# The end of an attention and quantised-feed-forward layer on one core: tiles moved ahead of the last values, and rounding and addition shared differently between GpSimd and VectorE

## What is computed

```python
def _quant_per_tensor(x):
    scale = jnp.maximum(jnp.max(jnp.abs(x)) / QMAX, EPS)
    q = jnp.clip(jnp.round(x / scale), -QMAX, QMAX).astype(jnp.int8)
    return (q, scale)
...
h = _dyn_quant_linear(hidden_state, w1, b1)
h = jax.nn.gelu(h, approximate=False)
return _dyn_quant_linear(h, w2, b2)
```

## Time and profile before

| what | value |
|---|---|
| median of 3 runs | 736.91 us |
| the profiled execution's own time | 732.62 us |
| its span, first to last instruction | 730.8 us |
| mean granted TensorE clock | 0.944 of full speed |
| busy: PE, DVE, ACT, POOL | 86%, 73%, 63%, 65% |
| last values done | about 675.8 us |
| first Gelu starts, last maximum ends | 677.56, 702.70 us |
| first rounding starts | 704.08 us |
| last addition on GpSimd ends | 728.17 us |

### The profile page before, as it was taken

How to read it: one execution, slowest core, us unless ns; L and a number is a source line. 1 busy time by engine, 2 the same in 40 slices (tenths; PEclk the granted TensorE clock), 3 DMA queues, 4 the chain that set the end, 5 groups by cost and what they waited for, 6 DMA issues and landing times.

```text
span 730.8 us, 15856 instructions
## 1 busy us (share of the span) xinstructions
PE 630.3 (86%) x6282; PEld 489.4 (67%) x6282; DVE 532.5 (73%) x822; ACT 461.5 (63%) x715; POOL 476.4 (65%) x256
## 2 busy tenths in 40 slices
PE   7989878878899899989987998789899988974956
PEld 5666656667686687667765776678677866863635
DVE  6746789766668786878677777676778777873896
ACT  3466746667657675767676667665677667663754
POOL 2488599775665887579768577855777778610225
PEclk9798998989999999999999999999899999997889
DMA  9866776688987988799888878888788888886003
GB/s 255 262 208 193 179 126 125 122 157 154 205 150 134 180 159 136 148 191 166 145 139 153 138 135 150 160 134 159 140 151 139 132 132 141 134 142 127 15 1 115
DMA packets 326680, 108.34 MB, mean 148 GB/s; under 512 B 308880, under 2 KB 317648, under 8 KB 326480
## 3 DMA queue, kind: packets, MB, share of 16 engines
q1 hardware_dynamic: 325824, 106.75, 75.5%
q10 hardware_dynamic: 784, 0.59, 0.3%
HBM read 21.30 MB, written 10.49 MB: 43 GB/s over the span
## 4 chain that ended last, share of the span: by engine, by line
PE 30%; DVE 28%; ACT 13%; DMA 12%; issue 11%; POOL 5%; SPq 1%; POOLq 0%; DVEq 0%; ACTq 0%
PE psum L1059 28%; DVE small L862 12%; DMA pt<-p_src 9%; ACT psum L678 7%; DVE p_src L870 5%; ACT p_src L672 3%; DMA acc<-in_L_attn_x 2%; ACT o_hi L660 2%; DVE o_lo L894 2%; DVE hid L1039 1%; DVE small L1008 1%; POOL res L533 1%; DVE acc L761 1%; DVE acc L900 1%; DVE o_norm L887 1%
## 5 line engine op out<-in xcount | busy, mean ns | idle before, releaser
L672 ACT ACTIVATE p_src<-psum,small 128x1024 f16<-128x1024 f32 (+7 forms) x256 | 183.4, 742 | 190.4 <-DVE small L862 189.8
L862 DVE TENSOR_REDUCE small<-psum 128x1 f32<-128x1024 f32 (+7 forms) x256 | 186.7, 750 | 58.6 <-PE psum L1059 58.4
L870 DVE TENSOR_TENSOR p_src<-psum,p_src 128x1024 f16<-128x1024 f32 (+2 forms) x192 | 182.5, 951 | 32.3 <-ACT psum L678 31.9
L1059 PE MATMUL psum<-kv_tok,pt 128*128 128x65 f16 (+1 forms) x3456 | 146.6, 198 | 52.5 <-DMA pt<-p_src 38.5
L1059 PEld LDWEIGHTS psum<-kv_tok,pt 128*128 128x128 f16 x3456 | 124.1, 100 | 97.2 <-issue 68.7
L678 ACT ACTIVATE psum<-psum,small 128x1024 f32<-128x1024 f32 (+7 forms) x256 | 178.2, 719 | 0.0
L1059 PE MATMUL psum<-k_hi,q_hi 128*128 128x512 f32 (+2 forms) x384 | 161.0, 419 | 15.8 <-POOL q_lo L484 6.3
L466 POOL TENSOR_TENSOR q_swap<-q_raw,sin_sb 32x1024 f32<-32x1024 f32 x32 | 75.9, 2373 | 119.4 <-ACT q_raw L606 118.9
L1059 PE MATMUL psum<-k_hi,q_lo 128*128 128x512 f32 (+2 forms) x384 | 134.7, 351 | 0.0
L1059 PE MATMUL psum<-k_lo,q_hi 128*128 128x512 f32 (+2 forms) x384 | 134.4, 350 | 0.0
L1059 PEld LDWEIGHTS psum<-k_hi,q_hi 128*128 128x128 f32 x384 | 76.5, 199 | 23.8 <-issue 11.1
(11 more groups left out here) (160 smaller groups left out, 918.5 us busy)
## 6 DMA issues: line engine op xcount, KB each, us to landing
pt<-p_src SPq DMA_TRANSPOSE x384, 3.3
wq_split<-w_split SPq DMA_DIRECT2D x4, 1024.0 KB, 5.0
k_rotated<-k_split SPq DMA_DIRECT2D x8, 512.0 KB, 3.4
wq<-wq_split SPq DMA_DIRECT2D x16, 256.0 KB, 3.4
acc<-in_L_attn_x SPq DMA_DIRECT2D x4, 512.0 KB, 7.9
ffn_t<-in_L_attn_W_o SPq DMA_DIRECT2D x1, 2048.0 KB, 19.5
k_hi<-k_rotated SPq DMA_DIRECT2D x8, 256.0 KB, 3.9
k_lo<-k_rotated SPq DMA_DIRECT2D x8, 256.0 KB, 4.6
```

Of the source, the lines that this page charges most:

```text
L672: ins = act.activation(p_src[u][:, 0, at:at + w], psum[:, COLS[i]:COLS[i] + w], ACT.Exp, bias=nb)
L862: dve.tensor_reduce(sm["mcol"][:, NT * (n % 2) + i:NT * (n % 2) + i + 1], psum[:, COLS[i]:COLS[i] + (i + 1) * P], AX.X, ALU.max, negate=True)\
L870: dve.tensor_tensor(p_src[u][:, 1, :], psum[:, o:o + WIDE[u]], p_src[u][:, 0, :], ALU.subtract)\
L1059: ins = pe.matmul(dst, lhs, rhs, start=start, stop=stop, skip_group_check=True)
```

## The change

- **Order of the tiles.** Half 0 first, c = 0 to 7, then half 1. The loop on TensorE now ends after iteration n = 31. The values of units 0 and 1 of the last step come first, then tile 0; units 2, 3, 4 and 5 come behind tiles 0, 2, 4 and 6 (`VALUES_BEHIND`), tile 0 of the queries behind tile 6. `normalise` of the last step is done after maximum 6 (`HEADS_AT`), together with the two small `dg` products. The last `turn_pair`s stand behind tiles 8 and 9 (were 0 and 1), the output products behind tiles 11, 12, 13, 14 (were 4, 6, 8, 10). Banks are given per tile, bank 5 only from tile 10 on. ScalarE waits for `att_pool` and `att_sp` before Gelu 0 (was Gelu 6).
- **Taking MAGIC off.** Parts (0,1) and (1,1) go from VectorE to GpSimd, behind its eight b2 additions.
- **Addition of `acc`.** GpSimd keeps the even results u, VectorE adds the odd ones itself, right behind their multiplication.

```diff
-OUT_AT = {4: 0, 6: 1, 8: 2, 10: 3}
-DVE_QUANT = {(0, 1), (1, 1)}
-FFN_ORDER = [(1, c) for c in (2, 3, 4, 5, 6, 7, 0, 1)] + [(0, c) for c in range(8)]
-FFN_BANKS = (0, 2, 5)
+OUT_AT = {11: 0, 12: 1, 13: 2, 14: 3}
+TURN_AT = {8: 0, 9: 1}
+VALUES_BEHIND = {0: 2, 2: 3, 4: 4, 6: 5}
+HEADS_AT = 6
+POOL_QUANT = {(0, 1), (1, 1)}
+FFN_ORDER = [(h, c) for h in range(2) for c in range(8)]
+FFN_BANKS = (0, 2, 6, 0, 2, 6, 0, 2, 0, 2, 5, 0, 2, 5, 0, 2)
...
+        def first_head(m):
+            return first_of_head if m + 1 < LAST else bank[4][:, 0:VC]
...
-                sp.wait_ge(S["f_res"], u + 1)
+                sp.wait_ge(S["f_res_dve" if u % 2 else "f_res"], u // 2 + 1)
...
             pool.wait_ge(S["f_bias"], TT // 2)
-            for u in range(TT // 2):
+            for i, (t, hf) in enumerate(sorted(POOL_QUANT)):
+                pool.wait_ge(S["f_round"], 2 * t + hf + 1)
+                cs = slice(4 * hf, 4 * hf + 4)
+                pool.tensor_scalar(hqs[t % 2][:, cs, :], hid_quarter(t)[:, cs, :], -MAGIC, None, ALU.add)\
+                    .then_inc(S["f_quant_pool"], 1)
+                pool.wait_ge(S["f_quant_pool"], i + 1)
+            for u in range(0, TT // 2, 2):
...
-                if i == 6:
+                if i == 0:
                     for s in ("att_pool", "att_sp"):
                         act.wait_ge(S[s], 1)
-                if i < 2:
-                    turn_high(1, i, MISC_END + i)
+                if i in TURN_AT:
+                    turn_high(1, TURN_AT[i], MISC_END + TURN_AT[i])
...
-                    if n and j == NS - 1:
+                    if 0 < n < LAST and j == NS - 1:
                         normalise(n - 1, False)
-            normalise(LAST - 1, True)
-            for k in range(2):
-                dve.tensor_scalar(dg[:, k, :], identf[:, :], sm["w2s"][:, k:k + 1], None, ALU.mult).then_inc(S["f_dg"], 1)
             for i in range(16):
                 dve.wait_ge(S["f_gelu"], i + 1)
                 ins = dve.tensor_reduce(sm["hmax"][:, i:i + 1], hid[:, FFN_ORDER[i][0], FFN_ORDER[i][1], :], AX.X, ALU.max,
                                        apply_absolute_value=True)
-                if i < 2:
-                    turn_low(1, i, TURNS[LAST] + i + 1, MISC_END + i)
+                if i == HEADS_AT:
+                    normalise(LAST - 1, False)
+                    normalise(LAST - 1, True)
+                    for k in range(2):
+                        dve.tensor_scalar(dg[:, k, :], identf[:, :], sm["w2s"][:, k:k + 1], None, ALU.mult)
+                if i in TURN_AT:
+                    turn_low(1, TURN_AT[i], TURNS[LAST] + TURN_AT[i] + 1, MISC_END + TURN_AT[i])
...
                 dve.tensor_tensor(res[u % RES][:, :, :], bank[u % 4].rearrange("p (t n) -> p t n", n=D), s2_row[:, :, :],
                                   ALU.mult).then_inc(S["f_mul"], 1)
+                if u % 2:
+                    dve.wait_ge(S["f_mul"], u + 1)
+                    dve.wait_ge(S["f_bias"], TT // 2)
+                    t = 4 * QUARTERS[u // 2] + 2 * (u % 2)
+                    y = res[u % RES]
+                    dve.tensor_tensor(y[:, :, :], y[:, :, :], acc[:, t:t + 2, :], ALU.add).then_inc(S["f_res_dve"], 1)
...
                     dve.tensor_scalar(h, h, sm["rsh"], MAGIC, ALU.mult, ALU.add).then_inc(S["f_round"], 1)
-                    if (t, hf) in DVE_QUANT:
-                        dve.wait_ge(S["f_round"], 2 * t + hf + 1)
-                        dve.tensor_scalar(hqs[t % 2][:, 4 * hf:4 * hf + 4, :], h, -MAGIC, None, ALU.add)\
-                           .then_inc(S["f_quant_dve"], 1)
...
-            for n in range(LAST + 1):
+            for n in range(LAST):
...
-            pe.wait_ge(S["lo_done"], NS * LAST)
+            for u in range(2):
+                values(LAST - 1, u)
             for i in range(16):
                 half, c = FFN_ORDER[i]
-                if i >= 3:
-                    pe.wait_ge(S["f_gelu"], i - 2)
-                if i == 2:
-                    pe.wait_ge(S["misc6_used"], BANK_OF.count(6))
+                taken = [k for k in range(i) if abs(FFN_BANKS[k] - FFN_BANKS[i]) < 2]
+                if i < 2:
+                    pe.wait_ge(S["lo_done"], NS * LAST - (2 if i == 0 else 0))
+                if i == 1:
+                    pe.wait_ge(S["head_read"], 2 * (LAST - 1))
+                if taken:
+                    pe.wait_ge(S["f_gelu"], taken[-1] + 1)
+                if i == FFN_BANKS.index(6):
+                    for b in (6, 7):
+                        pe.wait_ge(S[f"misc{b}_used"], BANK_OF[:MISC_END].count(b))
+                if i == FFN_BANKS.index(5):
+                    pe.wait_ge(S["head_read"], 2 * LAST)
...
-                if i < 2:
-                    turn_pair(i, MISC_END + i, 2 * end)
+                if i in VALUES_BEHIND:
+                    values(LAST - 1, VALUES_BEHIND[i])
+                    if i == HEADS_AT:
+                        first_values(LAST - 1)
+                if i in TURN_AT:
+                    pe.wait_ge(S["f_gelu"], 6)
+                    turn_pair(TURN_AT[i], MISC_END + TURN_AT[i], 2 * end)
```

More of the change, by code:

```diff
@@ L255, in build @@
             pool_step qhi_done qlo_done o_hi_done norm_step
-            att_pool att_sp f_quant_dve
-            f_psum f_gelu f_max f_hrow f_hall f_step f_att f_bias f_round f_quant f_out f_mul f_res f_s2 f_dg f_dgps""".split()
+            att_pool att_sp f_quant_pool
+            f_psum f_gelu f_max f_hrow f_hall f_step f_att f_bias f_round f_quant f_out f_mul f_res f_res_dve f_s2 f_dg f_dgps""".split()
         S = {n: sem(n) for n in names}
@@ L712, in _ @@
                 act.wait_ge(S["f_psum"], i + 1)
-                if i == 6:
+                if i == 0:
                     for s in ("att_pool", "att_sp"):
                         act.wait_ge(S[s], 1)
-                first = FFN_BANKS[i % 3] * CH
+                first = FFN_BANKS[i] * CH
                 act.activation(hid[:, half, c, :], psum[:, first:first + 2 * CH], ACT.Gelu,
                                scale=sm["s1"][:, c:c + 1], bias=sm["b1"][:, c:c + 1]).then_inc(S["f_gelu"], 1)
-                if i < 2:
-                    turn_high(1, i, MISC_END + i)
+                if i in TURN_AT:
+                    turn_high(1, TURN_AT[i], MISC_END + TURN_AT[i])
             for t in range(4):
                 for hf in range(2):
-                    if (t, hf) in DVE_QUANT:
+                    if (t, hf) in POOL_QUANT:
                         continue
@@ L873, in normalise @@
             def normalise(m, first):
-                part = first_of_head if first else rest_of_head
+                part = first_head(m) if first else rest_of_head
                 hb = part.rearrange("p (t c) -> p t c", c=VC)
@@ L1009, in _ @@
                                         apply_absolute_value=True)
-                if i < 2:
-                    turn_low(1, i, TURNS[LAST] + i + 1, MISC_END + i)
+                if i == HEADS_AT:
+                    normalise(LAST - 1, False)
+                    normalise(LAST - 1, True)
+                    for k in range(2):
+                        dve.tensor_scalar(dg[:, k, :], identf[:, :], sm["w2s"][:, k:k + 1], None, ALU.mult)\
+                           .then_inc(S["f_dg"], 1)
+                if i in TURN_AT:
+                    turn_low(1, TURN_AT[i], TURNS[LAST] + TURN_AT[i] + 1, MISC_END + TURN_AT[i])
                 if i in OUT_AT:
@@ L1225, in values_of @@
             def values_of(m, u, tile, at):
-                o = first_of_head if tile == 0 else rest_of_head[:, (tile - 1) * VC:tile * VC]
+                o = first_head(m) if tile == 0 else rest_of_head[:, (tile - 1) * VC:tile * VC]
                 for j in range(tile + 1):
@@ L1370, in _ @@
             end = LAST
-            pe.wait_ge(S["lo_done"], NS * LAST)
+            for u in range(2):
+                values(LAST - 1, u)
             for i in range(16):
                 half, c = FFN_ORDER[i]
-                if i >= 3:
-                    pe.wait_ge(S["f_gelu"], i - 2)
-                if i == 2:
-                    pe.wait_ge(S["misc6_used"], BANK_OF.count(6))
+                taken = [k for k in range(i) if abs(FFN_BANKS[k] - FFN_BANKS[i]) < 2]
[10 more added lines that the diff above has]
+                    pe.wait_ge(S["head_read"], 2 * LAST)
                 for h in range(2):
                     for k in range(2):
-                        mm(bank[FFN_BANKS[i % 3] + h], w1_t[:, k, c * P:(c + 1) * P],
+                        mm(bank[FFN_BANKS[i] + h], w1_t[:, k, c * P:(c + 1) * P],
                            qx_t[:, k, half * T + h * CH:half * T + (h + 1) * CH], k == 0, k == 1,
                            S["f_psum"] if h and k else None)
-                if i < 2:
-                    turn_pair(i, MISC_END + i, 2 * end)
+                if i in VALUES_BEHIND:
[5 more added lines that the diff above has]
+                    turn_pair(TURN_AT[i], MISC_END + TURN_AT[i], 2 * end)
```

(4 more changed lines are left out.)

## The result

The changed kernel took 740.74 us (median of 20 runs, 736.43 to 749.89) against 733.83 us before (20 runs, 729.59 to 739.44): ratio 1.0089, 95% interval 1.0068 to 1.0111. It is slower, by 0.9%; forecast were +7.7 us, 1.0%. Medians, here and in the experiments, are over all runs, but ratios and their intervals leave out runs counted as slow (over 1.5% above the fastest of their kernel; of the changed kernel the one of 749.89 us), so the two can differ a little.

What follows compares the result with a forecast made beforehand. The prediction took no single engine to bound the whole span, since the chain goes through every engine in turn. Its terms -0.9 + 2.1 + 6.5 gave +7.7 us, 744.6 us on the median, range 740 to 748.

Steps and rivals of the forecast that it cites:

- Stage A: All up to the last maximum: Gelu 0 starts earlier but most is lost again on TensorE, -0.9 us.
- half-clock case: Stage A with TensorE's clock at 1.2 GHz until about 679.9 despite tile 0 in the idle gap: -0.4 us.
- full-clock case: Stage A with TensorE's clock kept at 2.4 GHz by tile 0 in the idle gap: -1.5 us.
- Stage B: The scale, between last maximum and first rounding: held by GpSimd's late b2 additions, +2.1 us; 0 if not held.
- Line 1024 and the first rounding thus wait: Step in Stage B: b2 additions to 705.7 hold VectorE, so rounding starts 3.5 us behind maximum 15 instead of 1.4.
- Stage C: First rounding to the span's end: GpSimd parts of 5.38 us delay products and hold roundings, 33.6 against 27.1, +6.5 us.
- The sum: Whole kernel: the three stages' terms together, +7.7 us, 740.3 for the profiled execution, 744.6 on the median.
- Rival 1: GpSimd's part takes 2.0 us (fp32 rate): Stage C -0.3, sum +0.9, 737.8 us; chance 0.06.
- Rival 2: GpSimd's part takes 5.4 us but holds no rounding: Stage C +1.5, sum +0.6, 737.5 us; chance 0.06.
- Rival 3: GpSimd works truly beside VectorE, parts 2.0 us and unheld: sum -3.3, 733.6 us, faster; chance 0.05.
- Rival 4: Gelu 0 starts at 667, clock full: Stage A 4.8 us earlier still, sum +2.3, 739.2 us; no chance of its own.

Runs made afterwards that it cites:

- experiment 3: The changed kernel with parts (0,1) and (1,1) given back to VectorE; 737.08 us, ratio 1.0041 against the kernel before.
- experiment 1: The kernel before with only parts (0,1) and (1,1) moved to GpSimd for taking MAGIC off; 741.51 us, ratio 1.0107.
- experiment 2: The kernel before with only the odd results' additions of acc moved to VectorE; 734.71 us, ratio 1.0030.
- experiment 9: The changed kernel with GpSimd's two parts written as times 1.0 minus MAGIC; 735.38 us, ratio 0.9995 against the kernel before.
- experiment 10: The changed kernel with SyncE's signal att_sp given ahead of the last step's transposes; 735.84 us, ratio 1.0005 against the kernel before.
- 8: Run 7 with SyncE's signal att_sp given ahead of the last step's transposes; 726.00 us, ratio 0.9901 against the kernel before.
- 7: Experiment 3 with GpSimd's last four b2 additions each waiting for its own output addition; 732.33 us, ratio 0.9962 against the kernel before.

## Why the prediction was right

By its steps, against the stretches (forecast to measured):

- **Stage A, -0.9 (-0.4 or -1.5).** Measured -1.6 in the trace of after and -0.4 in that of experiment 3. The lower gain is the half-clock case, with the number worked out for it; but in both traces the clock was full from tile 1 on and fell anew in the stop in front of tile 3, where the prediction let the old fall at 666.2 go on. The full-clock case did not occur: -1.6 came with the clock low for 3.4 us, so its nearness to -1.5 is partly luck, and so is a mean of the two cases that lies between them. Gelu 0 starts 0.3 us behind SyncE's last issue, as said. Products behind tiles 11 to 14 bound TensorE at 2.3 us a tile, as said (VectorE idles 0.47 in front of maximum 15 in its row at 702.73, and as long in front of the two maxima before it).
- **Stage B, +2.1.** Measured +1.5, and not where it was put: the first rounding starts 1.55 us behind the end of maximum 15 (703.95 to 705.50), not 3.5, and the loss lies in the first two roundings, 3.83 instead of 2.48. The step that was mis-sized is "Line 1024 and the first rounding thus wait". The 128x1 product ran in 0.15 us at 705.11, inside the third b2 addition; a single element per partition wasn't held, where a 128x2 product had been. That brought the first rounding's request in front of the fourth addition, so that GpSimd stood in turn (5.90 for four), and only part of its work lay in VectorE's way.
- **Stage C, +6.5.** Here +7.5 for the parts (experiment 1) and -0.65 for the odd additions (experiment 2), +7.0 for both (after). Worked out by the same steps were 34.5 - 27.1 = 7.4 for the parts (put at 7.3 in the expectation of experiment 1) and 0.9 for the additions. The order in which the engines would take their turns came out as said: rounding (2,0) ahead of part (1,1), rounding (2,1) behind it, the addition on VectorE held 0.6 by GpSimd's (1.34).
- **The sum** +7.7 stands against +6.9 behind the mark and +6.9 between the medians. Part of this closeness is luck: A and B came out 0.7 and 0.6 lower than forecast, C 0.5 higher. In absolute time 740.74 is 3.9 us below the forecast 744.6 and near the lower end of its range, because the 736.91 that it was put on, the median of three runs, is 3.1 above the median of 20.
- **Rival 1** (2.0 us for a part) was wrong of this instruction and about right in its price: experiment 9 is that case, with -0.3 behind the mark where +0.9 was worked out; A and B came out 0.5 and 0.6 lower than the prediction's terms, and the last stage at -0.5 against -0.3. The estimate of 1.8 us by the Trainium skill (GPSIMD Engine Reference, Elementwise, as weighed in the prediction) is close to the 1.90 of the form with two operations, and a third of the 5.37 of the one with a single operation.
- **Rival 2** (long but nothing held) falls with experiment 1 and the rows of 5.79 and 6.38 us.
- **Rival 3** falls with it. A version faster than before existed all the same, but not by that way.
- **Rival 4** had no chance of its own, since `att_sp` comes behind SyncE; as a price it held in the sum: +2.3 worked out, +2.0 measured in experiment 10, where A was 0.4 and B 0.6 lower than its terms and C' 0.6 higher.

What stays open: how much of the 7.5 us is length and how much is the holding alone. The kernel in which GpSimd's part is long and no rounding stands beside it wasn't tried; by the prediction's steps (its rival 2) the last stage would grow by 1.5 us instead of 6.5. The prediction was right on the length of 5.4 us and didn't see its reason. It took it for what the output's type costs, and the two-operation row beside it, 1.1 us for half the elements, for the price of fp32; it was the count of operations.

## What to carry to other kernels

Before work goes to GpSimd, look for a row of exactly that instruction form, and time its neighbours in form too. Then, if VectorE has SBUF-to-SBUF work like the roundings beside it, lay the two one behind the other in the sum: here the 3.5 us by which a slow part was longer than a quick one counted in full, and nothing of it was hidden behind the roundings. And when tiles are pulled forward, follow every semaphore that the first consumer waits for: here one signal at the end of another queue, needed for loads long landed, was worth 5.1 us (experiment 10 against after) to 6.4 (8 against 7), more than all that the rest of the change gained.

## What the runs showed of the hardware

- On GpSimd a 128x2048 instruction of this kind with one operation takes 5.4 us (a subtraction of a constant in three pairs of types, a multiplication from fp32 to bf16), with two operations 1.9 to 2.0, a copy 1.89.
- A one-element-per-partition product on VectorE isn't held by GpSimd (0.15 us in the middle of an addition of 1.26), a two-element one was (1.42, ending with GpSimd's instruction, in a single row).
- An SBUF-to-SBUF rounding on VectorE in pieces of 3 and 5 rows of 512 takes 1.27 and 1.80 us against 1.24 for 4 rows: 3 rows cost as much as 4.
- TensorE's granted clock in the 7 us behind the same code was 0.51, 0.76 or 1.00 on average, and stage A followed it: 29.3 to 29.4, 28.2 to 28.4, 23.0 (the last one with Gelu 0 freed).
